# Slots without keys: next value weights issued before the tile stage's transfers, the gate first in the last batch's slot, the subtraction between scaling and turning

## The reference, cut to what matters

```python
# 32 sequences of 64 tokens, width 256
def step(state, inp):                              # 128 steps per sequence and head (2 keys per token)
    q_t, k_t, v_t, g_t, b_t = inp
    state = state * jnp.exp(g_t)[..., None, None]
    corr = jnp.einsum('bhk,bhkv->bhv', k_t, state)
    v_new = (v_t - corr) * b_t[..., None]
    state = state + jnp.einsum('bhk,bhv->bhkv', k_t, v_new)
    return state, jnp.einsum('bhk,bhkv->bhv', q_t, state)
# q, k, v: projection, depthwise convolution over 4 tokens, silu; q and k normalized
o = o * rsqrt(mean(o * o) + EPS) * o_norm_w * silu(x @ Wg.T)
x = layernorm(x + o @ Wo.T)                        # L0_attn
x = layernorm(x + cross_attention(x, ctx, seg))    # 16 heads, 64 keys, compressed keys and values
x = layernorm(x + ffn(x))                          # integer weights with scales, silu(gate) * up
```

## Time and profile before

| | us |
|---|---|
| median of 3 runs | 1129.11 (1126.56 to 1131.92) |
| the profiled execution | 1130.19 |
| its span | 1128.4 |
| slots without keys, 32 to 42 | about 570 to 730 |

### The profile page before, as it was taken

How to read it: one execution, slowest core, us unless ns; L and a number is a source line. 1 busy time by engine, 2 the same in 40 slices (tenths; PEclk the granted TensorE clock), 3 DMA queues, 4 the chain that set the end, 5 groups by cost and what they waited for, 6 DMA issues and landing times.

```text
span 1128.4 us, 29265 instructions
## 1 busy us (share of the span) xinstructions
PE 1075.7 (95%) x11676; PEld 757.7 (67%) x11676; DVE 852.7 (76%) x1420; ACT 692.8 (61%) x1243; POOL 470.0 (42%) x713
## 2 busy tenths in 40 slices
PE   8979799999999999999998999899999999999998
PEld 3444455655555565565554566689999899999987
DVE  5989778878879778779887756777677767777662
ACT  5778568777677776877866766534433444434434
POOL 1649575684783873873957512301000000001000
PEclk9999899999999999999998999999999999999999
DMA  4223445756666566675556452511222221111100
GB/s 133 50 70 79 101 65 101 118 121 114 124 118 118 126 135 146 136 138 103 77 91 219 109 152 67 183 44 48 53 53 54 54 72 48 48 48 48 29 21 15
DMA packets 168215, 102.37 MB, mean 91 GB/s; under 512 B 98416, under 2 KB 148720, under 8 KB 167184
## 3 DMA queue, kind: packets, MB, share of 16 engines
q1 hardware_dynamic: 166928, 100.30, 40.3%
q10 hardware_dynamic: 1152, 0.21, 0.1%
HBM read 63.24 MB, written 14.67 MB: 69 GB/s over the span
## 4 chain that ended last, share of the span: by engine, by line
PE 62%; DVE 15%; issue 7%; ACT 5%; DMA 4%; POOL 3%; SPq 3%; ACTq 0%; DVEq 0%; POOLq 0%
PE proj L611 13%; DVE conv L1248 6%; PE out L1840 5%; PE proj L1909 5%; PE turned_v_chain L1840 5%; PE turned_v_chain L1921 4%; PE proj L1779 4%; PE gram L626 3%; PE gram L1814 3%; DMA vg_weights<-in_vg_w 2%; PE out L635 2%; PE proj L1828 2%; DVE gram_decayed L1268 1%; PE decays L611 1%; PE decays L1828 1%
## 5 line engine op out<-in xcount | busy, mean ns | idle before, releaser
L611 PE MATMUL proj<-xT,vg_weights 128*128 128x512 f32 x384 | 193.8, 628 | 4.2 <-DMA vg_weights<-in_vg_w 3.2
L2175 POOL TENSOR_TENSOR rope<-rope_part,rope_part 128x512 f32<-128x512 f32 x32 | 40.0, 1270 | 321.6 <-DVE rope_part L2097 321.6
L1248 DVE SCALAR_TENSOR_TENSOR conv<-proj,kq_weights,conv 128x504 f32<-128x504 f32 (+2 forms) x195 | 141.3, 730 | 22.4 <-ACT conv L957 18.5
L1248 DVE SCALAR_TENSOR_TENSOR conv<-proj,vg_weights,conv 128x504 f32<-128x504 f32 (+2 forms) x192 | 139.4, 728 | 21.6 <-ACT conv L957 17.2
L1536 POOL TENSOR_TENSOR inverse<-inverse,rank_one 128x30 f32<-128x30 f32 (+14 forms) x240 | 133.2, 555 | 18.8
L611 PE MATMUL proj<-xT,kq_weights 128*128 128x512 f32 x260 | 126.0, 611 | 5.7 <-DVE conv L1248 5.0
L1533 POOL TENSOR_TENSOR rank_one<-inverse 128x30 f32<-128x30 f32 (+14 forms) x240 | 118.7, 495 | 23.0 <-DVE inverse L1310 8.0
L611 PEld LDWEIGHTS proj<-xT,vg_weights 128*128 128x128 f32 x384 | 66.6, 193 | 57.3 <-issue 49.9
L968 ACT ACTIVATE keys_q<-conv 128x512 f32<-128x512 f32 x96 | 63.9, 668 | 55.3 <-DVE conv L1248 54.1
L611 PEld LDWEIGHTS proj<-xT,kq_weights 128*128 128x128 f32 x260 | 45.3, 189 | 60.1 <-issue 43.2
L1248 DVE SCALAR_TENSOR_TENSOR conv<-decays,kq_weights,conv 128x504 f32<-128x504 f32 (+2 forms) x66 | 48.1, 729 | 39.3 <-ACT conv L957 37.7
(11 more groups left out here) (280 smaller groups left out, 2477.2 us busy)
## 6 DMA issues: line engine op xcount, KB each, us to landing
kq_weights<-in_kq_w SPq DMA_DIRECT2D x32, 390.0 KB, 6.6
vg_weights<-in_vg_w SPq DMA_DIRECT2D x32, 390.0 KB, 6.9
o_scratch<-oT SPq DMA_DIRECT2D x32, 256.0 KB, 2.5
o_in<-o_scratch SPq DMA_DIRECT2D x16, 512.0 KB, 4.2
o_rs<-o_rs_quarters SPq DMA_DIRECT2D x88, 64.0 KB, 6.1
diagonal<-gram_decayed SPq DMA_DIRECT2D x128, 32.0 KB, 2.0
inverse<-inverse SPq DMA_DIRECT2D x32, 128.0 KB, 2.8
q_first<-rope SPq DMA_DIRECT2D x128, 32.0 KB, 1.9
```

The source lines that it names most:

```text
L611: mm = e.matmul(bank(c, u)[:], w[:, (k * 3 + c % 3) * 128:(k * 3 + c % 3 + 1) * 128], xT[g][:, k, :], start=(k == 0), stop=(k == KD - 1))
L1248: e.scalar_tensor_tensor(acc(c, u)[:, :, back:], src[:, :, 0:S - back], weights(c, u)[:, j:j + 1], acc(c, u)[:, :, back:], ALU.mult, ALU.a ...
L2175: e.tensor_tensor(turned[half][:].rearrange("p b r q -> p r b q"), parts[2 * half][:], parts[2 * half + 1][:], op).then_inc(s_turned, 1)
```

## The change

- SP: from slot 32 on, the value weights of the unit after next are issued behind the store of `oT` and ahead of everything else in the slot, in place of the next unit's at the head of the slot. Slot 32 does both.
- W of unit 22 (slot 32) is scaled by VectorE in place of Pool.
- Y of unit 24 (slot 33) is copied by ScalarE in place of VectorE.
- Slot 33, VectorE: the gated output stands at the head of the slot, ahead of the convolution V0, in place of between the norms and the scaled rows.
- Slot 36, VectorE: `less_sum` stands between the scaled columns and `solve_turn`, in place of behind `solve_turn`.
- `softmax_sum` is cut in two; for tile 0 the sum goes to slot 41, the reciprocal and the product stay in slot 42.

```diff
--- before.py
+++ after.py
@@ -133,7 +133,6 @@
 SCANNED = U - LAG
 ROWS = ((GB * H, 3 * GB * H, 0), (3 * GB * H, U * GB, ROW))
 ROWS_SLOT = 5
-Y_BY_ACT = True
 POOL_STEPS = 3 + 14 + 4
 SOLVE = 13
 LOADED, NORMS, READY, K_NORM, TURNED, TURNED2 = 2, 3, 10, 11, 12, 13
@@ -302,7 +301,7 @@
         rope_slots = {last_slot - 2: 0, last_slot: 1}
         joined = lambda u: u + LAG < last_slot - 3
         quiet = lambda s: U < s <= last_slot - 4
-        w_by_vector = lambda s: U + 1 < s <= U + 4
+        w_by_vector = lambda s: s == U or U + 1 < s <= U + 4
         low_later = lambda u: joined(u + 1)
         high_chain = EB[:].rearrange("p (b s) -> p b s", b=GB)
         acc = lambda c, u: conv[place[c, u] % 4]
@@ -490,14 +489,14 @@
                 for s in range(SLOTS):
                     ua, ub, uc, uo = s, s - 1, s - LAG, s - LAG - 2
 
-                    def load_value_weights():
-                        if live(uc + 1) and uc >= 0:
-                            wait(e, s_conv[V1], 3 * uc)
-                            wait(e, s_proj[G], uc)
-                            e.dma_start(blob_c[(uc + 1) % 2][:], a["vg_w"][head(uc + 1)]).then_inc(d_wc[(uc + 1) % 2], 16)
-
-                    if s >= U:
-                        load_value_weights()
+                    def load_value_weights(u):
+                        if 0 < u < U:
+                            wait(e, s_conv[V1], 3 * (u - 1))
+                            wait(e, s_proj[G], u - 1)
+                            e.dma_start(blob_c[u % 2][:], a["vg_w"][head(u)]).then_inc(d_wc[u % 2], 16)
+
+                    if s == U:
+                        load_value_weights(uc + 1)
                     if live(uo) and by_rows(uo):
                         e.wait_ge(s_rs, uo + 1)
                         wait(e, s_gr, uo)
@@ -523,6 +522,8 @@
                         e.wait_ge(s_gr, uo + 1)
                         e.dma_start(o_scratch[:, 4 * group(uo):4 * group(uo) + 4, head(uo), :],
                                     oT[uo % 2][:].rearrange("v (t n) -> v t n", n=TILE)).then_inc(d_out[uo % 2], 16)
+                    if s >= U:
+                        load_value_weights(uc + 2)
                     if s == 1:
                         for tile, n in ((ones_mean, "ones_mean"), (onorm, "o_norm_w"), (guard, "guard")):
                             e.dma_start(tile[:], a[n]).then_inc(d_late, 16)
@@ -1111,6 +1112,8 @@
                         tap(Q, ub)
                     elif live(uc):
                         tap(V0, uc)
+                    if s == U + 1:
+                        copy_y(uc)
                     if live(uo):
                         e.wait_ge(s_norm, uo + 1)
                         if by_rows(uo):
@@ -1125,7 +1128,7 @@
                         e.activation(o_ln, o_ln, ACT.Exp, scale=-0.5).then_inc(s_rs, 1)
                     if s in rope_slots:
                         ahead["rsqrt"](0, rope_slots[s])
-                    if Y_BY_ACT and live(uc) and s <= U:
+                    if live(uc) and s <= U:
                         copy_y(uc)
                     if h is not None:
                         k_norms(h)
@@ -1381,7 +1384,7 @@
                     if s == 3:
                         beta_turned()
                     woven = LAG < s <= U
-                    if live(uc) and s > LAG and not (Y_BY_ACT and woven):
+                    if live(uc) and s > U + 1:
                         copy_y(uc)
                     loading, turning = (solve_at(s, n) if s > LAG else None for n in (5, 8))
                     h = solve_at(s, 7)
@@ -1416,7 +1419,7 @@
                         gate_w()
                     last_batch = loading is not None and s > U
 
-                    if live(uo) and not last_batch and not woven:
+                    if live(uo) and not woven:
                         gate_output()
                     if live(uc):
                         convolve(V0, uc)
@@ -1424,7 +1427,6 @@
                         solve_load(loading, 0)
                         solve_load(loading, 1)
                         solve_norms(loading)
-                        gate_output()
                         solve_scale_rows(loading)
                     if loading is not None and not last_batch:
                         solve_load(loading, 0)
@@ -1443,8 +1445,9 @@
                     if s == last_slot + 1:
                         ahead["sums"](0, 2)
                         ahead["normalize"](0, 2)
+                        ahead["softmax_total"](0)
                     if s == last_slot + 2:
-                        ahead["softmax_sum"](0)
+                        ahead["softmax_divide"](0)
                         ahead["turn_att"](0)
                         ahead["rope_parts"](2)
                     if live(ub) and not woven:
@@ -1468,12 +1471,12 @@
                                         ALU.mult).then_inc(s_wk, 1)
                     if turning is not None and s >= U:
                         solve_scale_columns(turning)
-                        if s > U:
-                            solve_turn(turning)
                     if quiet(s) and turning is None:
                         scale_output(uo)
                     if live(uc) and s > LAG and not live(ua) and not last_batch:
                         less_sum(uc)
+                    if turning is not None and s > U:
+                        solve_turn(turning)
                     if s >= LAG and live(ua):
                         conv_step(K1, ua, 2)
                         if live(uc) and s > LAG:
@@ -2073,14 +2076,20 @@
                     e.wait_ge(s_soft, 5 * u + 1)
                     e.tensor_tensor(rows, rows, wide(high[:]), ALU.subtract).then_inc(s_soft, 1)
 
-                def softmax_sum(u):
+                def softmax_total(u):
+                    e.wait_ge(s_exp, u + 1)
+                    e.tensor_reduce(total[:], att[u % 2][:], AX.X, ALU.add).then_inc(s_soft, 1)
+
+                def softmax_divide(u):
                     rows = att[u % 2][:]
-                    e.wait_ge(s_exp, u + 1)
-                    e.tensor_reduce(total[:], rows, AX.X, ALU.add).then_inc(s_soft, 1)
                     e.wait_ge(s_soft, 5 * u + 3)
                     e.reciprocal(total[:], total[:]).then_inc(s_soft, 1)
                     e.wait_ge(s_soft, 5 * u + 4)
                     e.tensor_tensor(rows, rows, wide(total[:]), ALU.mult).then_inc(s_soft, 1)
+
+                def softmax_sum(u):
+                    softmax_total(u)
+                    softmax_divide(u)
 
                 def turn_att(u):
                     if u == 0:
@@ -2165,7 +2174,7 @@
                             good_keys(u1)
 
                 return {"segments": segments, "good_keys": good_keys, "sums": sums, "normalize": normalize, "mask_scores": mask_scores,
-                        "softmax_max": softmax_max, "softmax_sum": softmax_sum, "turn_att": turn_att, "rope_parts": rope_parts, "dequantize": dequantize, "loop": loop}
+                        "softmax_max": softmax_max, "softmax_total": softmax_total, "softmax_divide": softmax_divide, "turn_att": turn_att, "rope_parts": rope_parts, "dequantize": dequantize, "loop": loop}
 
             def gpsimd(e):
                 def rope(u):
```

## The result

The changed kernel takes 1133.34 us (median; 1131.79 to 1135.38), the kernel before 1129.03 (1125.26 to 1131.92) beside it: a ratio of 1.0039 [1.0025, 1.0054]. That is slower by 0.4%, within the half percent that I called no change, and 2.3 us above the forecast. The profiled span grew from 1128.4 to 1131.5 us.

A forecast was written before the change was run, and what follows sets the result against it. TensorE, busy 95% of the span, was taken as the bound. -4.8 (upper pieces) +4.5 (lower pieces) +2.7 (clock) -0.5 (softmax) = +1.9 on 1130.19 gave 1132.1, or 1131.0 us as a median; range 1125.5 to 1137.

The forecast's parts named there:

- Slots 32 and 33: W, Y and early gate edits: columns' followers about 0.45 us earlier, gate 0.55 off the path, rows scaled 1.0 us earlier.
- Weights ahead of the bulk: Slot 35: unit 26's load issued at about 601.5, so the 2.8 us wait and the low clock behind it go.
- What is late next: Slot 36: Pool's elimination ends last at 635.5, then less_sum; chain_low(27) begins at 637.2 instead of 644.11.
- Upper pieces: Slot 36: store issued at 642.2, pieces landed 5.6 us later; chain_high(28) 4.8 us earlier, at 647.8.
- queue rival: Weights' data served first: upper pieces 1.5 us later, lower 1.4, clock falls before chain_high(28) too; 1136.6 us; chance 0.20.
- Lower pieces: Slot 37: pieces queue behind unit 30's load, waiting for G(28); TensorE idle 4.5 us before chain_low(28), bounds 3.7 to 5.9.
- The clock in slot 37: Clock falls behind the 4.5 us idle, costing 2.7 us; bounds 0 and 3.3.
- The end: Softmax sum moved to slot 41 shortens the wait for the turned attention: 0.5 us gained; bounds 0.5 lost to 3.4 won.
- the faster one: Clock stays high in slot 37, short landings: 1126.6 us, or 1123.7 with the low clock at 731.5 gone; chance 0.15.
- the gain of slot 35: Slot 35 shrinks by 5.5 us: 2.8 us of weights' wait and 2.7 of low clock.

The follow-up runs named there:

- the loads alone: Kernel before with only the moved weight loads (SP's new order), no other edits: 1135.60 us, ratio 1.0063.
- less_sum behind the turning: less_sum put back behind solve_turn: in the changed kernel 1134.67 us, ratio 1.005; in the fastest version 1124.85 us, ratio 0.9967.
- the fastest version: Changed kernel with the lower pieces (slot 37) and upper pieces (slot 36) both issued ahead of the loads: 1121.77 us, ratio 0.9937.
- the fastest version's repeat: Second run of the same kernel, both pairs of pieces ahead of the loads: 1122.36 us, ratio 0.9945.
- the first experiment: Changed kernel with only the lower pieces in slot 37 issued ahead of the load of unit 30: 1123.69 us, ratio 0.9956.
- the gate back: Fastest version with slot 33's gate back between the norms and the scaled rows: 1122.85 us, ratio 0.9946.
- the old order back: Changed kernel with SP's old order of loads in the late slots, all other edits kept: 1124.23 us, ratio 0.996.

## Why the prediction was right, and where it was not

The trace gives -4.7 (upper pieces) + 1.6 (clock in slot 36) + 5.1 (lower pieces) + 4.2 (clock in slot 37) - 0.2 (slots 38 to 41) - 3.4 (softmax and tail) + 0.5 (a longer idle before the output projection, 1.17 for 0.64) = +3.1, against a forecast of +1.9 that had the same order of causes.

- **Slots 32 and 33.** Confirmed in part. The columns in slot 32 took 1.23 us beside an idle Pool, for 1.86. The rows in slot 33 were scaled at 595.10, 2.5 us earlier and not 1.0, since the diagonal was there 1.8 us earlier (591.15 for 592.95) where I had some 0.45: its transfers were issued 0.4 us earlier, and the slowest of the four landed 2.6 us after its issue for 4.0 before. From there to the rows it took 3.95 us for 4.64, which is the gate's 0.55 and a little more. Only part of that is the change: the slowest landing is between 2.3 and 4.0 us over all runs, and the diagonal's issue in the kernels with this VectorE code between 586.5 and 589.4, so the rows were scaled between 595.0 and 598.6 there. The gate's 0.55 us are seen in the trace; in the time, the run that undoes it shows no difference.

```profile
581.46 1.23 DVE L1319 TENSOR_TENSOR inverse<-inverse,rho 128x1024 f32<-128x1024 f32 x1
...
591.15 2.02 DVE L1293 STREAM_TRANSPOSE inverse<-diagonal 128x512 f32<-128x512 f32 x2 [0.67 <-DMA diagonal<-gram_decayed]
...
595.10 1.22 DVE L1313 TENSOR_TENSOR inverse<-inverse,rho 128x1024 f32<-128x1024 f32 x1
```

- **Weights ahead of the bulk.** Right. The load went out at 600.07, the wait of slot 35 is gone, its clock 1.00.
- **What is late next: Pool's elimination, then less_sum.** Right. Pool ended at 634.42 (635.5 forecast), `chain_low(27)` waited 2.26 us for less_sum and ran at 636.24 (637.2 forecast).
- **Upper pieces.** The sum was right by two errors that cancel, which is luck. (The forecast's own times, 647.8 against 652.69, give 4.9 and not 4.8, and the lower bound of the landing, 4.6, should be 4.4 by the terms it names.) The store went out 1.1 us earlier than I said (641.10 for 642.2), because the elimination was earlier; from store to landing it was 6.8 us where I took 5.6. The term failed at "the data in the queue is the same": the order is not, and the pieces landed 4.0 to 5.1 us after their issue instead of 2.6 and 4.4. My queue rival had just this, to be decided at about 7 us; at 6.8 its fall of the clock came, for 1.6 us instead of the 2.7 it was given.
- **Lower pieces.** The mechanism was right, to the matmul that waits and to what is queued ahead: 5.13 us for a forecast of 4.5, within its bounds of 3.7 and 5.9. The 0.3 us for the weights' data ahead was too small. The run with the pieces behind the wait but ahead of the data measures it at 1.2.
- **The clock in slot 37.** It fell as said, but the price was 4.2 us, outside my bounds of 0 and 3.3. I had taken the fall's length from one row (6.6 us after a wait of 2.85, of which the row shows 6.1); here the clock was low for 10.2 us. This is the largest error of the sum. The other falls behind waits of 4.8 and 5.1 us were as long or longer (10.2 us in the loads alone, 13.6 with less_sum behind the turning); why a longer idle brings a longer fall is open.
- **The end.** I took 0.5 us with a bound of 3.4; the bound came true, since the low clock went with 1.26 us of idle (1.82 to 0.56). The run with the sum back in slot 42 shows that the split does this. I had this low clock down as something that might go by luck, and it should have been priced like the others: the idle before it was the thing that the edit shortened.

The forecast's 1131.0 came close because +1.5 of clock, +0.6 of waiting and +1.6 of a fall I had left to the rivals stood against -2.9 in the tail; that leaves 1.2 us in the spans (with +0.3 in slots 38 to 41 and ahead of the output projection, and +0.1 of the upper pieces), and the medians lie another 1.1 us further apart than the spans (+4.2 for +3.1 against the median that I started from): the profiled execution of the kernel before was 1.1 us above its median, that of the changed kernel at its median. That the sum came within 2.3 us is thus partly luck. The case that happened is between the forecast and the queue rival, and its tail is that of the faster one. What the sum got right is that the gain of slot 35 is given back at the one matmul that follows the event on which the moved load waits (4.7 us gained there, 5.1 lost); the sign was then left to the clock (1.6 and 4.2 lost, about 2.7 of the 3.4 won).

Left open: why the low clock in slot 37 lasts 10.2 us; why the slowest landing of the diagonal varies by 1.7 us. Where the clock falls is itself not the same in every execution: of the 11 runs of the fastest version's repeat the mean granted clock was 0.989 to 0.994, with 0.989 and 0.991 in the two slowest. So the prices of single falls above hold for the executions shown. The loads alone also had an idle of 1.8 us before the mix but no low clock behind it, where the kernel before had one, so that fall depends on more than the idle's length. W by VectorE in slot 32 and Y's copy by ScalarE in slot 33 weren't tried by themselves. Undone one at a time in the fastest version, less_sum's place (2.5 to 3.1 us by the medians) and the softmax's split (1.7 to 2.2) make together 4.2 to 5.3 us, about the 4.8 that the edits other than SP's give alone; that they add up is an estimate.

## What to carry to other kernels

A DMA issue that waits for a semaphore stops everything behind it on its in-order queue. Before moving one forward, list the issues that it is moved past, and see whether the user of any of them runs right behind the event that the moved one waits for; here two pieces of 128 KB were held for a load that nobody needed for a slot, and putting the pieces first turned +0.4% into -0.6%. Short transfers with a user close by go ahead of bulk whose user is far, also when both could be issued at once: in slot 37 the order alone was 1.2 us of landing. An idle of a busy TensorE should be costed at its length plus the low clock that may follow: 5.1 us of wait cost 9.3, while waits of 1.6 to 2.6 us were followed by a low clock in some executions and not in others.

## What the runs showed of the hardware that I had not expected

- Two pieces of the inverse (128 KB each, within the on-chip memory) landed 3.7 to 5.1 us after their issue wherever 390 KB of weights stood directly ahead of them on the same queue. With the weights behind them it was 2.6 to 2.9 in some executions, but the second piece took 4.1 to 4.5 in others (4.4 in the kernel before, 4.2 in the second run of the fastest version); no run takes the weights away, so whether they are the cause isn't shown. Issued 1.9 us after the weights, in the first run of the fastest version, they took 3.7 to 4.1; issued 4.5 us after them, in the first experiment, 2.8 to 2.9.
- In the slots from 33 on and at the mix the clock fell around each of the eight waits of 2.85 us and more. Behind shorter ones it was irregular: it fell behind 2.4 us in slot 36 of the changed kernel, behind 1.86 in the first experiment and behind 2.3 in the second run of the fastest version, and it stayed at 1.00 behind 2.56 us with less_sum behind the turning, behind 2.2 with the gate back and behind 2.0 with the old order back. The low stretches lasted 3.4 us at the least; those of 10.2 us and, once, 13.6 us came with waits of 4.8 and 5.1 us.
- The fall in slot 36 (3.4 us) took 1.6 us of time and that in slot 37 (10.2 us) 4.2: a low clock costs half of its stretch at most, and less where TensorE had slack.
